# A graph network kernel on one core: transfers that add into the output, the last norm moved up, four fetches ahead of the scatters, registers read ahead of a loop

## What is computed

```python
h = jnp.maximum(_layernorm(x), 0.0)
# layer 0: mean over incoming edges, twice, then a norm with gamma and beta
h1 = relu(mean_aggregate(h) @ W1l.T + h @ W1r.T + b1)
h2 = mean_aggregate(h1) @ W2l.T + h1 @ W2r.T + b2 + h
x = x + layernorm(h2) * gamma + beta
# layer 1: attention over edges and one loop per node, 4 heads of 32
h = jnp.maximum(_layernorm(x), 0.0)
x_l = h @ W
logits = leaky_relu(a_src[src] + a_dst[dst] + a_edge, 0.2)
p = exp(logits - segment_max(logits, dst)[dst])
out = segment_sum(p / segment_sum(p, dst)[dst] * x_l[src], dst) + bias
x = x + out
```

## Time and profile before

| | us |
|---|---|
| median of three executions | 3653.07 (3652.0 to 3653.54) |
| the profiled execution | 3650.43 |
| its span, first to last instruction | 3648.6 |
| PE busy | 3008.9 (82%) |
| DVE busy | 2621.2 (72%) |
| POOL busy | 1916.9 (53%) |
| ACT busy | 1003.6 (28%) |

### The profile page before, as it was taken

The page is one execution under the profiler, slowest core; times in us unless marked ns, Lnnn a source line. Parts: engine busy times, 40 slices in busy tenths (PEclk is TensorE's granted clock), DMA queues, the critical chain, the costliest instruction groups (busy, mean ns, idle before and its releaser), DMA issues. The chain is left out here.

```text
span 3648.6 us, 66680 instructions
## 1 busy us (share of the span) xinstructions
PE 3008.9 (82%) x21816; PEld 2406.5 (66%) x21816; DVE 2621.2 (72%) x7475; ACT 1003.6 (28%) x2323; POOL 1916.9 (53%) x1960
## 2 busy tenths in 40 slices
PE   5799999999999999888777777777777777777773
PEld 5566666777765566567666666666766666766663
DVE  4789999996687544477666766666766666766667
ACT  4455555664200011122222222112222122222210
POOL 5420010161102233177777777777777777777771
PEclk9999999999999999966666666666666666666666
DMA  5233333473278788532222222222222222222224
GB/s 170 85 144 140 137 132 142 159 169 129 65 231 228 217 243 251 167 93 55 56 55 55 56 55 56 55 55 55 55 55 55 55 56 55 56 55 55 54 55 120
DMA packets 148342, 381.45 MB, mean 105 GB/s; under 512 B 39094, under 2 KB 83054, under 8 KB 139618
## 3 DMA queue, kind: packets, MB, share of 16 engines
q0 software_dynamic: 61360, 127.21, 17.6%
q1 hardware_dynamic: 48694, 222.47, 16.8%
q10 hardware_dynamic: 37916, 27.15, 2.5%
HBM read 258.39 MB, written 119.89 MB: 104 GB/s over the span
## 5 line engine op out<-in xcount | busy, mean ns | idle before, releaser
L1968 POOL DMA_INDIRECT G<-x_tab,idx x1611 | 1532.2, 951 | 504.9 <-issue 490.7
L2057 PE MATMUL pu<-MSG,OH 128*128 128x140 f32 x3282 | 626.2, 353 | 2.7 <-DVE ACC L2151 2.6
L2151 DVE TENSOR_TENSOR ACC<-pu,ACC 128x140 f32 x1641 | 484.9, 295 | 135.3 <-PE pu L2057 88.0
L923 PE MATMUL psR<-SPL,AE 128*128 128x384 bf16 x3038 | 570.7, 329 | 0.0
L2057 PEld LDWEIGHTS pu<-MSG,OH 128*128 128x128 f32 x3282 | 559.3, 246 | 6.2 <-issue 2.3
L1652 PE MATMUL psR<-SPL,AE 128*128 128x384 bf16 x3038 | 510.7, 328 | 4.2 <-PEq L213 2.3
L1988 ACT COPY OHT<-pt 128x512 f32<-128x512 f32 (+1 forms) x432 | 236.6, 558 | 958.1 <-PE pt L2033 957.2
L890 ACT CAST AE<-psA 128x784 bf16<-128x784 f32 x496 | 397.6, 813 | 316.3 <-PE psA L913 315.7
L2046 PE MATMUL px<-ADG,OHT 128*128 128x4 f32 x3240 | 464.9, 270 | 0.0
L2046 PEld LDWEIGHTS px<-ADG,OHT 128*128 128x128 f32 x3240 | 436.8, 212 | 10.3
L1652 PEld LDWEIGHTS psR<-SPL,AE 128*128 128x128 bf16 x3038 | 297.1, 98 | 196.5 <-issue 6.8
(11 more groups left out here) (412 smaller groups left out, 3532.6 us busy)
## 6 DMA issues: line engine op xcount, KB each, us to landing
a_tab<-AE SPq DMA_DIRECT2D x62, 1568.0 KB
AE<-a_tab SPq DMA_DIRECT2D x60, 800.0 KB, 6.3
AE<-a_tab SPq DMA_DIRECT2D x60, 768.0 KB, 6.3
G<-x_tab,idx POOLq DMA_INDIRECT x1611
at_in<-in_edge_attr SPq DMA_DIRECT2D x26, 250.0 KB
room<-in_edge_attr ACTq DMA_DIRECT2D x24, 250.0 KB
x_tab<-H ACTq DMA_DIRECT2D x13, 264.0 KB, 5.4
x_keep<-X ACTq DMA_DIRECT2D x13, 256.0 KB, 3.4
```

The source lines that it names most:

```text
L923: mm = pe.matmul(psR[:, i % 2, 0:3 * D], A[i % 2][:, h, :], SPL[:, h].rearrange("p s f -> p (s f)"), start=(h == 0), stop=(h == N_BLK - 1))
L1968: pool.indirect_dma_start(G[:, u % 4, j, :], None, x_tab, bass.IndirectOffsetOnAxis(ap=idx[:, u % 4, j:j + 1], axis=0)).then_inc(s_g[u % 4 ...
L2057: mm = pe.matmul(pu[:, k[0], k[1]:k[1] + MW], OH[:, u % 4, j, :], MSG[:, u % 2, j, :], start=True, stop=True)
L2151: dve.tensor_tensor(a, pu[:, k[0], k[1]:k[1] + MW][:, None, :], a, ALU.add).then_inc(s_c, 1)
```

## The change

1. `count_sums`: POOL issues fetches 0 to 3 first; the scatters follow from tile 0 on, and their wait and the `TT` transfer behind them; from fetch 4 on the order is as before.
2. `product_and_norm`: after the loop DVE begins normed(12) first and does turned(11) inside it, between the two norms' statistics of the first half and the product with gamma (`between`). `store` handles only the blocks that a quad has, so the last one copies and stores one block, not four; the rows that are no longer written are set to zero once. For quads 0 to 9, `keep` writes to `out`, not to `x_keep`. `x_tab` has 49 blocks of rows, not 52.
3. `attention`: both reads of block numbers after the loop move ahead of it, into registers of their own (`end`).
4. `finish`: for quads 0 to 9 (`ADDED = 10`), POOL issues a transfer that adds A to what lies in `out`. DVE's addition X + A, the load of X and the store of X go for them. A has room for all quads. The transfers count on a semaphore `s_pq`, taken once for the whole kernel and shared with the `TT` transfer.

```diff
@@ count_sums, POOL
+                def sources(f):
+                    if f >= 4:
+                        pool.wait_ge(s_kb, f - 3)
+                    pool.indirect_dma_start(srows[:, f % 4, :], None, flat_s, bass.IndirectOffsetOnAxis(
+                        ap=EKI[:, fetched[f]:fetched[f] + 1], axis=1)).then_inc(s_g[f % 4], 16)
+                for f in range(4):
+                    sources(f)
                 for i, t in enumerate(order):
                     if t == N_BLK:
                         pool.wait_ge(s_eo, 1)
-                    if i == first[of[i]]:
...
-                    if i >= 3 and done < N_BLK:
+                    if i == first[of[i]] and of[i] >= 4:
+                        sources(of[i])
+                    if done < N_BLK:
@@ product_and_norm, ACT
-                    act.dma_start(x_keep[:, QUAD * q:QUAD * q + QUAD, :], X[:, q % 3]).then_inc(s_xk[q % 3], 16)
+                    if q < ADDED:
+                        act.dma_start(kept[:, QUAD * q:QUAD * q + QUAD, :], X[:, q % 3]).then_inc(s_xk[q % 3], 16)
+                    else:
+                        act.dma_start(x_keep[:, QUAD * q:QUAD * q + QUAD, :], X[:, q % 3]).then_inc(s_xk[q % 3], 16)
...
-                    act.dma_start(tab[:, QUAD * q:QUAD * q + QUAD, :], H[:, QUAD * q:QUAD * q + QUAD, :]
-                                  ).then_inc(s_xt, 16)
+                    act.dma_start(tab[:, blocks(q), :], H[:, blocks(q), :]).then_inc(s_xt, 16)
@@ product_and_norm, DVE
                     scales(dve, c, st, ms[:], nv[:], rs[:, 0], sh[:, 0], sd[:], s_v, s_a, s_r, 2 * q)
+                    if between is not None:
+                        between()
                     dve.wait_ge(s_z, q + 1)
...
-                    for n in range(2):
-                        dve.tensor_copy(H[:, QUAD * q + 2 * n:QUAD * q + 2 * n + 2, :], o[:, n, :, 0:XW])
-                    for n in range(2):
-                        last = dve.tensor_copy(ADST[:, QUAD * q + 2 * n:QUAD * q + 2 * n + 2, :], o[:, n, :, XW:])
+                    halves = [(QUAD * q + 2 * n, min(QUAD * q + 2 * n + 2, N_BLK), n) for n in range(-(-width(q) // 2))]
+                    for low, high, n in halves:
+                        dve.tensor_copy(H[:, low:high, :], o[:, n, 0:high - low, 0:XW])
+                    for low, high, n in halves:
+                        last = dve.tensor_copy(ADST[:, low:high, :], o[:, n, 0:high - low, XW:])
...
+                dve.memset(ADST[:, N_BLK:], 0.0)
+                dve.memset(SELF[:, N_BLK:], 0.0)
...
-                turned(NQ - 2)
-                normed(NQ - 1)
+                normed(NQ - 1, between=lambda: turned(NQ - 2))
                 store(NQ - 2)
@@ attention, DVE
+                end = [None] * 16
+                blocks(N_GRP - 2, 8, end)
+                blocks(N_GRP - 1, 0, end)
                 blocks(-2, 0)
                 sums(-2, -2, range(8))
...
                 messages(N_GRP - 1, UN - 1, END)
-                blocks(N_GRP - 2, 8)
+                blk[:] = end
                 sums(N_GRP - 2, UN - 2, range(8, J))
-                blocks(N_GRP - 1, 0)
                 scale(c, N_GRP - 1)
@@ finish
+            @block.gpsimd
+            def _(pool):
+                for q in range(ADDED):
+                    pool.wait_ge(s_s, q + 1)
+                    pool.dma_start(o[:, blocks(q), :], A[:, blocks(q), :], accum_op=ALU.add).then_inc(s_pq, 16)
+                pool.wait_ge(s_pq, 16 + 16 * ADDED)
...
                 weigh(0)
                 for q in range(NQ):
-                    if q >= 1:
+                    if q - 1 >= ADDED:
                         finish_quad(q - 1)
                     add(q)
                     if q + 1 < NQ:
                         weigh(q + 1)
...
-                for q in range(NQ):
-                    sp.dma_start(X[:, blocks(q), :], x_keep[:, blocks(q), :]).then_inc(s_x[q], 16)
-                for q in range(NQ - 1):
-                    sp.wait_ge(s_d, q + 1)
-                    sp.dma_start(o[:, blocks(q), :], X[:, blocks(q), :]).then_inc(s_t, 16)
+                for q in range(ADDED, NQ):
+                    w = blocks(q).stop - blocks(q).start
+                    sp.dma_start(X[:, QUAD * (q - ADDED):QUAD * (q - ADDED) + w, :], x_keep[:, blocks(q), :]
+                                 ).then_inc(s_x[q], 16)
+                for q in range(ADDED, NQ - 1):
+                    sp.wait_ge(s_d, q - ADDED + 1)
+                    sp.dma_start(o[:, blocks(q), :], X[:, blocks(q - ADDED), :]).then_inc(s_t, 16)
```

More of the change, by code:

```diff
@@ L149, in sem @@
                     return h
+        s_pq = top.enter_context(nc.semaphore("p_q"))
+        kinds[s_pq.num] = True
         src_pad = nc.dram_tensor("src_pad", [E_PAD], I32).ap()
@@ L748, in count_sums @@
             s_sc = sem("c_sc", at, gathers=True)
-            s_tb = sem("c_tb", at, gathers=True)
+            s_tb = s_pq
             s_lm = sem("c_lm", at)
@@ L1274, in build @@
         stage(hidden)
+        ADDED = 10
         def product_and_norm(at, block):
@@ L1373, in product_and_norm @@
             tab = x_tab.rearrange("(b p) f -> p b f", p=P)
+            kept = out[0:full * P].rearrange("(b p) f -> p b f", p=P)
             order = list(range(N_BLK, NSL)) + list(range(N_BLK))
@@ L1682, in whole, with normed @@
                     dve.tensor_copy(RP[:, o % 2], psC[:, 0:D]).then_inc(s_rp, 1)
-                def normed(q):
+                def normed(q, between=None):
                     w = width(q)
@@ L2140, in blocks @@
                         skip_runtime_bounds_check_because="a block's number counts blocks begun so far, less one")
-                    blk[at_:at_ + 8] = v
+                    if to is None:
+                        blk[at_:at_ + 8] = v
+                    else:
+                        to[at_:at_ + 8] = v
                 def sums(g, u, chunks):
@@ L2301, in finish @@
             ex = sb("ex", [P, 2, NB, HEADS], F32, at)
-            A = sb("A", [P, 3, QUAD, D], F32, at)
+            A = sb("A", [P, NB, D], F32, at)
             B = sb("B", [P, 3, QUAD, D], F32, at)
-            X = sb("X", [P, NB, D], F32, at)
+            X = sb("X", [P, NB - QUAD * ADDED, D], F32, at)
             H = sb("H", [P, NB, XW], F32, at)
+            full = N_BLK - 1
+            o = out[0:full * P].rearrange("(b p) f -> p b f", p=P)
             Hh = H[:].rearrange("p b (h c) -> p b h c", h=HEADS)
@@ L2348, in pieces @@
                     w = blocks(q).stop - blocks(q).start
-                    return A[:, q % 3, 0:w], B[:, q % 3, 0:w]
+                    return A[:, blocks(q)], B[:, q % 3, 0:w]
                 def weigh(q):
@@ L2380, in _ @@
             def _(sp):
-                full = N_BLK - 1
-                o = out[0:full * P].rearrange("(b p) f -> p b f", p=P)
-                for q in range(NQ):
-                    sp.dma_start(X[:, blocks(q), :], x_keep[:, blocks(q), :]).then_inc(s_x[q], 16)
-                for q in range(NQ - 1):
-                    sp.wait_ge(s_d, q + 1)
-                    sp.dma_start(o[:, blocks(q), :], X[:, blocks(q), :]).then_inc(s_t, 16)
-                sp.wait_ge(s_d, NQ)
-                sp.dma_start(out[full * P:, :], X[0:TAIL, full, :]).then_inc(s_t, 16)
-                sp.wait_ge(s_t, 16 * NQ)
+                for q in range(ADDED, NQ):
+                    w = blocks(q).stop - blocks(q).start
+                    sp.dma_start(X[:, QUAD * (q - ADDED):QUAD * (q - ADDED) + w, :], x_keep[:, blocks(q), :]
[3 more added lines that the diff above has]
+                    sp.dma_start(o[:, blocks(q), :], X[:, blocks(q - ADDED), :]).then_inc(s_t, 16)
+                sp.wait_ge(s_d, NQ - ADDED)
+                sp.dma_start(out[full * P:, :], X[0:TAIL, full - QUAD * ADDED, :]).then_inc(s_t, 16)
+                sp.wait_ge(s_t, 16 * (NQ - ADDED))
         stage(finish)
```

17 lines of the change are left out of this document (6 added, 11 removed).

## The result

Twelve executions of the changed kernel have a median of 3642.93 us (3639.49 to 3646.3), twelve of the kernel before on the same chip 3652.01 us (3646.59 to 3653.76). The ratio is 0.9978, 95% interval 0.9970 to 0.9985: 8 us gained by the ratio, 9 by the medians. The forecast was 3635.1 us, a gain of 18. The profiled execution took 3642.7 us with a span of 3640.9.

The account below looks back on a forecast made before the run. PE bounds counting, POOL's gathers the attention stage, DVE the last stage. Gains of 7.1 + 3.7 + 2.6 + 4.6 = 18.0 us from the median 3653.07 give 3635.1 us; low end 3633.1 less 2 us for spread, high end 3646.

Parts of the forecast that it names:

- Four fetches: Counting stage: fetches 0 to 3 issued ahead of the scatters remove DVE's wait for the fourth; 7.1 us gained.
- a new wait of 2.1 us: Counting: DVE wants fetch 4 at 209.1, it lands at 211.24; 1.96 us are covered, so 0.2 us charged.
- What POOL does before fetch 4 keeps its sum: Counting: two fetches put ahead move the scatters 2.5 us later, but fetch 4 is still issued at 208.14.
- The old stall of 7.3 us: Counting, kernel before: PE's loss over the wait for the fourth fetch, 4.2 us idle and 3.1 slow.
- Rival (a): Counting: the wait moves to fetch 4, landing 6.4 us after issue; 6.4 us of gain lost, 3641.5 us; chance 0.12.
- Last norm, one block stored: End of product stage: norm begins earlier, 2.8 us; smaller last store, 0.5 and 0.4; sum 3.7 us, bounds 2.1 and 4.0.
- Registers: Attention tail: two reads of block numbers moved ahead of the loop; 2.6 us gained, bounds 1.4 and 2.7.
- Adding transfers: Last stage: ten DVE additions go, POOL's ten transfers at 2.4 us each set the end; 4.6 us gained.
- (b): Last stage: POOL's path sets the end at 4.1 us a transfer; 3652.1 us, no change; chance 0.12 including T 3.4 to 4.9.
- (c): Last stage: DMA engines add row after row, slower than before; at 6 us a quad 3671 us; chance 0.06.
- (d): Last stage: DVE locks POOL out of making transfers until DVE is done; 3658.7 us in all; chance 0.03.
- last sign of failure: Counting: the prediction fails if PE stalls anew for a fetch.

Follow-up runs that it names:

- g3: The kernel before, unchanged, run once more for another trace of its counting stage; 3649.09 us, one execution.
- g1: The changed kernel, but SyncE stores tile 6 only when fetch 4 has landed; 3634.23 us, ratio 0.9966 to the kernel before.
- e3: The changed kernel with fetch 4 issued after 26 of the 49 scatters; 3626.8 us, ratio 0.9945 to the kernel before.
- e4: The changed kernel with A of the next quad between B and A + B in the last stage; 3636.14 us, ratio 0.9969 to the kernel before.
- e2: The changed kernel with the order of fetches of the kernel before; 3637.41 us, ratio 0.9972 to the kernel before.
- f2: The changed kernel with fetch 4 behind 26 scatters and the next quad's A between B and A + B; 3625.28 us, ratio 0.9938 to the kernel before.

## Why the prediction failed, step by step

- **Four fetches, "a new wait of 2.1 us", "I charge 0.2".** This step failed. I had both the place and the reason of the new wait, and sized it by two numbers of the old order. "What POOL does before fetch 4 keeps its sum": it grew by 5.4 us. The 49 scatters took 4.5 us more, of which 2.2 are one scatter of 3.40 us. The rest goes with DVE, which was idle for 6 us in the old order while POOL scattered and now works beside it: in the old trace six scatters ran beside no one-hots, in the new one a single one, and those that did take 1.18 and 1.21 us on the mean. In g3 a scatter takes 0.97 us beside an idle DVE and up to 1.38 beside its one-hots. The Trainium skill (SBUF — State Buffer, Who interferes with whom) says that a DVE instruction with two SBUF inputs contends with a GpSimd instruction that reads SBUF; the one-hots are such, and the trace agrees; no run changed DVE's work alone. The wait for the scatters grew by 1.3 us, and the four fetches took 0.4 less. And "lands 3.1 us later": it landed in 6.4, since it now met the store of tile 6 (g1). 5.4 + 3.3 = 8.7 us of lateness turn the 2.1 us into 10.8; measured are 10.6.
- **The old stall of 7.3 us.** It was read rightly, from the one of six traces that was not like the others. Over six traces the old order's stage has a mean of 751.0 us, so there were 10 us to gain, and e3 gained them; the change as made gained none: its four traces have 751.4. The timed comparison of the fetches alone says +0.2 to +1.9 thousandths, 0.7 to 7 us; the traces say +0.4. That it is no gain is shown; its loss is only bounded.
- **Rival (a)** was the right mechanism with the wrong price. It took the landing of 6.4 us but left POOL's issue at 208.14, and so gave back 6.4 of 7.1 us; with both changed it gives back all and 3.5 more. Its chance of 0.12 was set by "fetch 4 itself landed in 3.1 us". That landing was measured with the store 1.6 us behind it, and the change moved the one without the other.
- **Last norm, one block stored, 3.7 us.** Measured 3.5 from the last sum to the first gather, by other shares: that the sum came out is partly luck, and so is the 3.6 us of the whole stage in the table, which varies by 9 us from trace to trace. The norm gave 1.8, not 2.8: POOL's addition to X (1.28 us) now falls on DVE's step L120, which took 1.12 us in the place of 0.16. The same rule of the Trainium skill covers it (two SBUF inputs against a reading GpSimd), and the trace agrees: L120 ends as POOL's addition does, in all twelve traces with this part. The smaller last block gave the rest: the store is issued 0.55 us earlier on DVE's side, and from it to the first gather it takes 3.2 us and not 4.3, 1.1 gained where I took 0.4.
- **Registers, 2.6 us.** Measured 2.7 to 3.0 in every trace with the part; the cost ahead of the loop, a first sum 1.35 us later where I had 1.2 at most, stayed hidden. The first of the reads there takes 2.06 us, which I had taken as 1.83.
- **Adding transfers, 4.6 us.** Measured 4.7, but by another route. I had POOL's path set the end at 2.4 us a transfer; it takes 1.28, and is hidden. DVE sets the end, and it gave 4.7 and not 6.0 because the addition X + A used to cover the end of B: without it A + B starts 0.12 us later, ten times. e4 shows this. Rivals (b), (c) and (d) did not come: 1.28 us a transfer, a median landing of 5.2 us (7.4 for the first, 4.3 to 4.6 for the last four, where I had taken 3.1), and no lock-out, as POOL was idle for 0.65 us ahead of each transfer and waited for DVE's sum.
- **The sum** would have been 11.0 for the last three parts against a forecast of 10.9. So the miss is the first part, which lost 3.5 us in this pair of traces where 7.1 were to be gained; the prediction's own last sign of failure, a new stall of PE for a fetch, came. That 3642.9 us still lie below its high end of 3646 is luck: that end was set by slow adding transfers, and there were none.

## What to carry to other kernels

- When a wait for a transfer is removed, the next transfer of that queue is the new limit, and its issue and landing must be worked out anew: what else is issued in the same microseconds, and which engine that stood idle now works beside the queue's owner.
- A small transfer that others wait for should be issued well ahead of a large periodic store (1.6 us was enough here, 0.7 was not), or the store held back behind it (g1, 3.7 us for one wait on SyncE's queue). Better still, put it ahead of work with slack (e3, 10 us).
- One trace is one execution. A stall whose length depends on how two queues happen to fall against each other should be read from several.

## What was not expected of the hardware

- **A small fetch is tied to a large store.** 64 KB of indirect reads land in 2.5 to 3.7 us, or together with a 1568 KB store's end, 5.9 to 7.5 us after the store's issue. The Trainium skill (DMA: Bandwidth & Descriptors, Queues, rings and completion order) says that a semaphore increment lands only after every earlier write from that DMA engine, across its queues. That rule alone does not make what is seen here: in the trace of the changed kernel 4.7 us after the fetch's issue its data had not begun to move either, and it moved as the store came to its end (the rows by DMA queue above). What held the packets back, no run here shows.
- **Scatters of 3.40 us** (in e2 one of 4.48) among those of 0.97 to 1.5: one or two in every trace but the first of before and the four of the slow chip, near one of three spots in POOL's queue. What is issued at the spot does not matter: in f2 it is fetch 4 itself that takes 3.41 us. Later in the counting stage five gathers (out of `r_tab`) take 4.47 to 4.48 us, the same five places in POOL's queue in all fourteen traces. The cause was not found.
- **POOL issues a direct adding transfer** of 128 partitions and 512 rows in 1.28 us, beside a DVE that is busy throughout. Four times the rows of a gather cost 1.35 times its 0.95 us, so the line through the earlier trace rows, 3.4 ns a row, did not hold.
